# Keys stacked with their remainder, row statistics on ScalarE, and GpSimd's normalisation steps moved to the end of attention

## The reference

```python
x = x + tanh(g_xattn) * xattn(layernorm(x), ctx, Wq, Wk, Wv, Wout, bout)   # 32 x 256 tokens x 256, 8 heads of 64
x = x + tanh(g_ffn)   * ffn(layernorm(x), Wg, W1, W2, Ws1, Ws2)            # 16 experts, the best 2 of each token
# xattn, for each of the 32 batches and 8 heads; ctx is 77 x 192
sim  = (x @ Wq) @ (ctx @ Wk).T * 64 ** -0.5
out  = softmax(sim) @ (ctx @ Wv)                                            # then out @ Wout + bout
```

## Time and profile before

| | us |
|---|---|
| median of three runs | 1064.97 |
| the profiled execution's own time | 1065.26 |
| its span in the profile | 1063.4 |
| `prepare`, to the first score matmul | 34.5 |
| attention, to the first instruction of `mix` | 477 |
| `mix` and `passes` | 552 |

### The profile page before, as it was taken

The page is one execution under the profiler, slowest core; times in us unless marked ns, Lnnn a source line. Parts: engine busy times, 40 slices in busy tenths (PEclk is TensorE's granted clock), DMA queues, the critical chain, the costliest instruction groups (busy, mean ns, idle before and its releaser), DMA issues. The chain is left out here.

```text
span 1063.4 us, 21220 instructions
## 1 busy us (share of the span) xinstructions
PE 939.3 (88%) x6806; PEld 868.9 (82%) x6807; DVE 799.2 (75%) x1833; ACT 470.1 (44%) x965; POOL 518.6 (49%) x681
## 2 busy tenths in 40 slices
PE   4799999999999999899699999988887787887873
PEld 3699999999999999898588888876877775877873
DVE  5699999999999999867589898884565552665553
ACT  4456565556555555443454445531333231433331
POOL 7546454544536364634334555442455553355554
PEclk9799999999999999989899999999999999999997
DMA  8213232222323212211525444448899962766650
GB/s 222 69 44 98 86 98 83 66 79 86 98 86 98 69 53 65 66 54 51 169 74 180 161 170 160 159 164 275 295 310 309 314 213 99 250 202 217 207 169 13
DMA packets 108327, 150.95 MB, mean 142 GB/s; under 512 B 21830, under 2 KB 72394, under 8 KB 108240
## 3 DMA queue, kind: packets, MB, share of 16 engines
q1 hardware_dynamic: 92880, 107.60, 33.6%
q0 software_dynamic: 15360, 42.24, 10.5%
HBM read 90.19 MB, written 65.90 MB: 147 GB/s over the span
## 5 line engine op out<-in xcount | busy, mean ns | idle before, releaser
L639 POOL TENSOR_TENSOR prob<-prob,row_sum 128x616 f32<-128x616 f32 x64 | 78.0, 1219 | 127.4 <-DVE row_sum L846 127.0
L75 PE MATMUL ps_h<-w_flat,eyT_hi 128*128 x320 | 97.7, 305 | 34.2 <-DVE eyT_lo L1607 28.3
L1488 POOL DMA_INDIRECT rows_scratch<-prow x80 | 78.9, 986 | 86.1 <-DVE prow L1625 67.9
L1488 POOL DMA_INDIRECT out<-prow x80 | 78.9, 986 | 82.0 <-DVE prow L1625 62.6
L1582 ACT ACTIVATE eyT_hi<-ps_ey 128x512 fp32r<-128x512 f32 x80 | 48.2, 602 | 128.5 <-PE ps_ey L1510 102.0
L1075 POOL DMA_INDIRECT rows_scratch<-row,slot x64 | 67.7, 1058 | 76.0 <-DVE row L1326 61.3
L1625 DVE TENSOR_TENSOR prow<-ps_z,prow 128x512 f32<-128x512 f32 x80 | 54.9, 686 | 57.6 <-PE ps_z L77 39.8
L75 PEld LDWEIGHTS ps_h<-w_flat,eyT_hi 128*128 128x128 f32 x320 | 61.3, 192 | 40.9 <-issue 40.9
L76 PE MATMUL ps_h<-w_flat,eyT_hi 128*128 x320 | 90.3, 282 | 0.0
L77 PE MATMUL ps_h<-w_flat,eyT_lo 128*128 x320 | 90.1, 281 | 0.0
L249 POOL TENSOR_TENSOR xT_lo<-xT_raw,xT_hi 128x512 fp32r<-128x512 f32 x32 | 41.2, 1288 | 94.5 <-ACT ctxb_hi L215 93.4
(11 more groups left out here) (269 smaller groups left out, 3389.3 us busy)
## 6 DMA issues: line engine op xcount, KB each, us to landing
prow<-rows_scratch SPq DMA_DIRECT2D x160, 258.0 KB
rows_scratch<-blank SPq DMA_DIRECT2D x34, 258.0 KB, 2.8
xT_raw<-in_xT SPq DMA_DIRECT2D x32, 256.0 KB, 4.5
x_tok<-in_x SPq DMA_DIRECT2D x32, 256.0 KB, 2.9
x_scratch<-x_tok SPq DMA_DIRECT2D x32, 256.0 KB, 3.2
row<-x_scratch SPq DMA_DIRECT2D x16, 512.0 KB, 4.0
x_ahead<-in_x SPq DMA_DIRECT2D x26, 256.0 KB, 4.5
w_raw<-in_W SPq DMA_DIRECT2D x16, 256.0 KB, 3.4
```

What stands on the lines that cost most here:

```text
L75: nc.tensor.matmul(out, lh, rh, start=start and n == 0, stop=False)
L639: nc.gpsimd.tensor_tensor(pr, pr, row_sum[i][:, :].unsqueeze(2).broadcast_to((P, H, CK)), ALU.mult).then_inc(normed, 1)
L1488: pool.indirect_dma_start(dram, bass.IndirectOffsetOnAxis(target, 0), row[u][:, i, 0:columns], None, bounds_check=bound, oob_is_err=False) ...
```

## The change

1. **Stacked keys.** `kT[j]` holds, for head j of the pair, the high part in that head's 64 rows and the remainder in the other 64 rows. The high query weight is now present in both halves of the rows, so one matmul gives high by high plus high by low. The low query weight keeps its zeros and gives low by high. A unit is two matmuls instead of three.
2. **Keys split in halves.** `high_K` becomes two ScalarE copies of 64 x 308, and `low_K` two VectorE subtractions of 64 x 308.
3. **Weights in `prepare`.** ScalarE makes four 64 x 1024 copies into the high query weight where it made two; one of GpSimd's two zero fills goes.
4. **Row statistics on ScalarE.** The two `bn_stats` of a batch of x ahead go. ScalarE makes the negated mean with an accumulating Identity (after `high_OT`) and the sum of squares with an accumulating Square (after `high_PT(b,0)`), 2 of each in a batch. GpSimd's chain for these groups has 15 steps instead of 20.
5. **Second normalisation.** The 23 steps at the end of group 6 and the 23 at the end of group 7 become one run of 23 steps over 60 tiles, behind all of GpSimd's attention work.

```diff
@@ query_keys
-    products(nc, out, [
-        (c.wq_hi[:, h, cc * P:(cc + 1) * P], c.wq_lo[:, h, cc * P:(cc + 1) * P],
-         kT[0][:, :], kT[1][:, :])]).then_inc(a.M_done, 1)
+    h, cc, both = 2 * pair + k // 2, k % 2, kT[k // 2][:, :]
+    nc.tensor.matmul(out, c.wq_hi[:, h, cc * P:(cc + 1) * P], both, start=True, stop=False)
+    nc.tensor.matmul(out, c.wq_lo[:, h, cc * P:(cc + 1) * P], both, start=False, stop=True).then_inc(a.M_done, 1)
+def half(j):
+    return slice(j * DH, (j + 1) * DH)
+def high_keys(nc, a, kT, bank):
+    for j in range(2):
+        high(nc, kT[j][half(j), :], bank[half(j), :], a.K_hi)
+def low_keys(nc, v, a, n, kT, bank):
+    for j in range(2):
+        v.wait_ge(a.K_hi, 2 * n + j + 1)
+        low(nc, kT[j][half(1 - j), :], kT[j][half(j), :], bank[half(j), :], a.K_lo)
@@ make_M
-    pe.wait_ge(a.K_lo, n + 1)
+    pe.wait_ge(a.K_lo, 2 * n + 2)
@@ prepare, GpSimd
-                for w in (c.wq_hi, c.wq_lo):
-                    nc.gpsimd.memset(f32(w[:, :, :]), 0.0).then_inc(zeroed, 1)
+                nc.gpsimd.memset(f32(c.wq_lo[:, :, :]), 0.0).then_inc(zeroed, 1)
@@ prepare, TensorE
+                pe.wait_ge(wq_hi_done, 4)
                 pe.wait_ge(wq_lo_done, 2)
@@ prepare, ScalarE
-                act.wait_ge(zeroed, 2)
                 act.wait_ge(centred, 4)
-                for j in range(2):
-                    high(nc, head_rows(c.wq_hi, j), wq_raw[j * DH:(j + 1) * DH, :, :], wq_hi_done)
+                for at in (0, 1):
+                    for j in range(2):
+                        high(nc, head_rows(c.wq_hi, j, j ^ at), wq_raw[half(j), :, :], wq_hi_done)
@@ attend, GpSimd, body
                     if exists(g + 2):
                         pool.wait_ge(ahead_stats, 2 * GB * (g + 1))
-                        rstd_of(2 * GB * (g + 2), 2 * GB, LN_STEPS * (g + 1))
-                    else:
-                        part = g - (GROUPS - 2)
-                        begin, end = 0 if part == 0 else known2, known2 if part == 0 else TILES - LATE_TILES
-                        pool.wait_ge(x1_stats, end)
-                        norm_of_stats(nc.gpsimd, linked(pool, rstd_chain, LN_STEPS * (GROUPS - 1) + NORM_STEPS * part),
-                                      c, begin, end - begin, var2[:, 0:end - begin], work2[:, 0:end - begin])
+                        tiles = slice(2 * GB * (g + 2), 2 * GB * (g + 3))
+                        rstd_of_squares(nc.gpsimd, linked(pool, rstd_chain, LN_STEPS + LN_AHEAD_STEPS * g),
+                                        squares[:, tiles], c.rstd1[:, tiles], var1[:, 0:2 * GB], work1[:, 0:2 * GB])
+                        pool.sem_inc(rstd_ready, 1)
@@ attend, GpSimd, behind the groups
+                pool.wait_ge(x1_stats, known2)
+                norm_of_stats(nc.gpsimd, linked(pool, rstd_chain, LN_STEPS + LN_AHEAD_STEPS * (GROUPS - 2)), c, 0, known2, var2[:, :], work2[:, :])
@@ attend, ScalarE
+                def mean_ahead(b, b_half, par):
+                    act.wait_ge(a.ahead_in[par], 16 * (b_half + 1))
+                    for i in range(2):
+                        t = 2 * (b + 2 * GB) + i
+                        nc.scalar.activation(unused[i][:, :], a.x_ahead[par][:, i, :], ACT.Identity, scale=-1.0 / D,
+                                             accum_out=less_mean[:, t:t + 1]).then_inc(ahead_mean, 1)
+                def squares_ahead(b, par):
+                    wait(act, ahead_stats, 2 * b)
+                    for i in range(2):
+                        t = 2 * (b + 2 * GB) + i
+                        act.wait_ge(ahead_mean, 2 * b + i + 1)
+                        nc.scalar.activation(unused[2 + i][:, :], a.x_ahead[par][:, i, :], ACT.Square,
+                                             bias=less_mean[:, t:t + 1],
+                                             accum_out=squares[:, t:t + 1]).then_inc(ahead_stats, 1)
...
                         if not (first and q == 0):
                             high_OT(b - 1)
+                        if exists(g + 2):
+                            mean_ahead(b, 2 * g + q // 2, q % 2)
                         if not last:
                             high_M_units(b, g, q, 1)
                         exponentials(b, 1)
                         high_PT(b, 0)
+                        if exists(g + 2):
+                            squares_ahead(b, q % 2)
@@ attend, VectorE: stats_ahead and its two calls in a batch
-                    nc.vector.bn_stats(a.stats1[:, bass.ds((2 * (b + 2 * GB) + i) * 6, 6)],
-                                       a.x_ahead[par][:, i, :]).then_inc(ahead_stats, 1)
```

More of the change, by code:

```diff
@@ L106 @@
 LN_STEPS = 6 + 2 + 3 * 4
+LN_AHEAD_STEPS = 1 + 2 + 3 * 4
 NORM_STEPS = LN_STEPS + 3
@@ L120, in linked, with newton @@
     return link
+def newton(g, link, rstd, var, work):
+    link(g.tensor_scalar(rstd.bitcast(I32), var.bitcast(I32), -0.5, float(SEED), ALU.mult, ALU.add))
+    link(g.tensor_scalar(var, var, -0.5, None, ALU.mult))
+    for _ in range(3):
+        link(g.tensor_tensor(work, rstd, rstd, ALU.mult))
+        link(g.tensor_tensor(work, work, var, ALU.mult))
+        link(g.tensor_scalar(work, work, 1.5, None, ALU.add))
+        link(g.tensor_tensor(rstd, rstd, work, ALU.mult))
 def rstd_by_newton(g, link, stats, rstd, var, work):
@@ L130, in rstd_by_newton, with rstd_of_squares @@
     link(g.tensor_tensor(var, var, work, ALU.add))
[L131 to L137, removed]
+    newton(g, link, rstd, var, work)
+def rstd_of_squares(g, link, squares, rstd, var, work):
+    link(g.tensor_scalar(var, squares, 1.0 / D, LN_EPS, ALU.mult, ALU.add))
+    newton(g, link, rstd, var, work)
 def norm_of_stats(g, link, c, first, tiles, var, work):
@@ L155, in attention_tensors @@
     a.ctxM = [sb("ctxM_hi", [P, 2, GK], F32R), sb("ctxM_lo", [P, GK], F32R)]
-    a.kT = [sb(f"kT_{s}", [P, GK], F32R) for s in ("hi", "lo")]
+    a.kT = [sb(f"kT_{j}", [P, GK], F32R) for j in range(2)]
     a.ctxb_raw = [sb(f"ctxb_raw{i}", [P, 2, CK]) for i in range(2)]
@@ L289, in high_K @@
     wait(act, a.M_done, 4 * n)
-    high(nc, a.kT[0][:, :], a.ps_proj[1][:, 0:GK], a.K_hi)
+    high_keys(nc, a, a.kT, a.ps_proj[1][:, 0:GK])
 def low_K(nc, v, a, n):
-    v.wait_ge(a.K_hi, n + 1)
-    low(nc, a.kT[1][:, :], a.kT[0][:, :], a.ps_proj[1][:, 0:GK], a.K_lo)
+    low_keys(nc, v, a, n, a.kT, a.ps_proj[1][:, 0:GK])
 def M_out(a, s, parity, cc, h):
@@ L334, in prepare @@
         bank_M = [ps(f"ps_m{i}", [P, 512])[:, 0:GK] for i in range(4)]
-        kT = [a.kT, [sb(f"kT2_{s}", [P, GK], F32R) for s in ("hi", "lo")]]
+        kT = [a.kT, [sb(f"kT2_{j}", [P, GK], F32R) for j in range(2)]]
         wq_raw = sb("wq_raw", [P, 4, D])
@@ L354, in by_batch, with head_rows @@
             return bank.rearrange("p (b k) -> p b k", b=GB)
-        def head_rows(w, j):
-            return w[j * DH:(j + 1) * DH, :].rearrange("p (q j) d -> p q j d", j=2)[:, :, j, :]
+        def head_rows(w, j, at=None):
+            return w[half(j if at is None else at), :].rearrange("p (q j) d -> p q j d", j=2)[:, :, j, :]
         with nc.Block(no_gpsimd_drain=True) as block:
@@ L430, in key_unit @@
                 def key_unit(n):
-                    wait(pe, a.K_lo, n - 1)
+                    wait(pe, a.K_lo, 2 * (n - 1))
                     keys(nc, c, a, bank_K[n % 2], n)
                 def query_key_units(n):
-                    pe.wait_ge(a.K_lo, n + 1)
+                    pe.wait_ge(a.K_lo, 2 * n + 2)
                     for k in range(4):
@@ L466, in high_key @@
                     wait(act, a.M_done, 4 * (n - 1))
-                    high(nc, kT[n % 2][0][:, :], bank_K[n % 2] if n < 4 else a.ps_proj[1][:, 0:GK], a.K_hi)
+                    high_keys(nc, a, kT[n % 2], bank_K[n % 2] if n < 4 else a.ps_proj[1][:, 0:GK])
                 def high_query_keys(n):
@@ L499, in _ @@
                                             ALU.subtract, ALU.mult).then_inc(centred, 1)
+                v.wait_ge(zeroed, 1)
                 for j in range(2):
@@ L512, in low_key @@
                 def low_key(n):
-                    v.wait_ge(a.K_hi, n + 1)
-                    low(nc, kT[n % 2][1][:, :], kT[n % 2][0][:, :], bank_K[n % 2] if n < 4 else a.ps_proj[1][:, 0:GK],
-                        a.K_lo)
+                    low_keys(nc, v, a, n, kT[n % 2], bank_K[n % 2] if n < 4 else a.ps_proj[1][:, 0:GK])
                 def low_query_keys(n):
@@ L554, in attend @@
         var1, work1 = sb("var1", [P, 4 * GB]), sb("work1", [P, 4 * GB])
+        less_mean, squares = sb("less_mean", [P, TILES]), sb("squares", [P, TILES])
+        unused = [sb(f"unused{i}", [P, D], BF16) for i in range(4)]
         ps_proj = a.ps_proj
@@ L572, in attend @@
         x1_done, x1_stats = sem("x1_done"), sem("x1_stats")
-        ahead_stats, rstd_chain, rstd_ready = sem("ahead_stats"), sem("rstd_chain"), sem("rstd_ready")
-        known2 = 2 * GB * (GROUPS - 2)
+        ahead_mean, ahead_stats, rstd_chain, rstd_ready = (
```

(2 more changed lines are left out.)

14 lines of the change are left out of this document (5 added, 9 removed).

## The result

| | before | changed |
|---|---|---|
| median | 1063.33 us (1060.57 to 1066.9, 4 runs) | 1052.16 us (1051.0 to 1053.72, 4 runs) |
| ratio, 95% interval | | 0.9897 [0.9864, 0.993] |
| the profiled execution, its span | 1065.26, 1063.4 | 1053.72, 1051.7 |

The change gains 11.2 us. The forecast was 20.6, and 1052.16 lies just past the range's high end of 1052.

What follows compares the result with a forecast made beforehand. TensorE's sum of starts was taken to bound attention, VectorE close behind. Units -15.4, batch 28 -6.0 and start +0.8 gave -20.6 us from 1065.26: 1044.7, stated as 1044.5 for the median; range 1040 to 1052.

Steps and rivals of the forecast that it cites:

- the second adds 0.39: VectorE's key split in attention: the second subtraction costs 0.39 us a batch, lower bound half of that.
- without them it is 4.78 us: VectorE between a batch's two `row_max`: 5.40 us less TensorE-caused waits is 4.78; 0.28 late, with 0.33 in hand.
- Rival (a): Attention loop: VectorE becomes the bound, loop 14.0 to 14.2 us, 4 to 10 us of gain lost, 1049 to 1054; chance 0.12.
- TensorE shows idle time before `attend_values`: Sign in the attention loop's profile that the forecast is wrong and VectorE has become the bound; no size given.
- Part 1: Attention units on TensorE: two matmuls instead of three save 0.573 us a batch, giving TensorE alone a 13.84 us period.
- Part 4: Row statistics on ScalarE in attention: both pairs, 1.1 us each, fit holes of 1.90 and 2.29 us; cost 0.
- rival (b): ScalarE's accumulating activations cost double: loop 14.4 us in 24 batches, 12 us lost, 1057 us; chance 0.04.
- Rival (d): ScalarE in attention: a table load at each turn between Exp and Square, 1075 us or some 1106; chance 0.04.
- The removal is worth nothing now: VectorE in attention: dropping the two `bn_stats` a batch gains nothing, as their cost lay in idle time.
- Part 5: Batch 28: with the normalisation chain gone it falls from 18.92 to 12.90 us, 6.0 us saved.
- rival (c): Batch 28's boundary wait stays, because `norm(28,0)` is late for another reason: 1050.7 us; chance 0.04.
- +0.8: Start, in `prepare`: five second key subtractions on VectorE cost between 0 and 1.9 us, taken as 0.8.

Runs made afterwards that it cites:

- halves in place: Changed kernel with both half-height key subtractions writing a spare tile in the rows they read, so remainders miss the products: 991.69 us, batch 13.99.
- same-rows version: Changed kernel with both key subtractions on rows 0 to 63 into two spare tiles, so no key remainder reaches the products: 981.93 us, batch 13.85.
- GpSimd moving the halves: Changed kernel with one full-height VectorE key subtraction, four half copies on GpSimd, statistics steps spread over three batches: 1038.91 us, batch 13.84.
- first group: Four runs of the change in parts, three rounds, sharing one chip with runs of the kernel before, which took 1007.73 us there.
- part 5 alone: Kernel before with only the single 60-tile normalisation chain behind GpSimd's attention work: 1001.15 us, ratio 0.9957, batch 28 at 12.83 us.

## Why the prediction was wrong

**Failed: part 2, "the second adds 0.39".** The term was mis-sized; it had a bound below (half of it) and none above, and the truth lay above. I argued from durations by columns, which are right (0.47 for 64 x 308), but the price of an instruction is the distance of starts, and that rests on the overlap with its neighbours. The pair and its neighbours take 0.75 more than the one subtraction did, not 0.39: worked out from the table, 0.39 for the second instruction and 0.36 for three lost overlaps. In `prepare` it can be read directly, between the same neighbours, first in the kernel before and then in the changed one:

```profile
25.74 0.41 DVE L509 BATCH_NORM_STATS2 stats<-xs 128x6 f32<-128x256 f32 x1
26.07 0.46 DVE L220 TENSOR_TENSOR kT_lo<-ps_k,kT_hi 128x308 fp32r<-128x308 f32 x1
26.45 0.74 DVE L534 TENSOR_SCALAR wo_raw<-wo_raw,tanh_g 128x1024 f32<-128x1024 f32 x1
```

```profile
27.69 0.42 DVE L537 BATCH_NORM_STATS2 stats<-xs 128x6 f32<-128x256 f32 x1
28.14 0.98 DVE L232 TENSOR_TENSOR kT<-ps_k,kT 64x308 fp32r<-64x308 f32 x2
29.15 0.75 DVE L560 TENSOR_SCALAR wo_raw<-wo_raw,tanh_g 128x1024 f32<-128x1024 f32 x1
```

From `bn_stats` to what follows the keys it is 0.71 us with one subtraction and 1.46 with two. In the loop, the own time of the second half is 9.12 us measured, 8.99 forecast; the rest of that half was 0.23 less than I had (8.99 + 0.36 - 9.12), so the two errors partly cancel.

**Failed: part 2, "without them it is 4.78 us".** I took the first half of the batch as VectorE's own work and let it end 0.28 late at the batch's start and catch up. It can't catch up: the scores of the second rows stand in TensorE's queue behind `attend_values`, which waits for VectorE's `PT_lo`. So when VectorE is late, the scores are late too. The distance stays at 5.02 with 0.34 of waiting in it (279.91 + 0.68 = 280.59, `attend_values` at 280.64, `row_max` at 285.53). My "0.33 in hand" were not to be had. The loop that sets the period now is `PT_lo`, `attend_values`, the second scores, VectorE's second half, `PT_lo`: 5.02 + 9.12 = 14.14, against TensorE's 13.84. With 5.0 for the first half, 13.84 leaves VectorE's second half 8.84, and the forecast's own 8.99 was already over that. The run with halves in place shows it: its second half takes just 8.99 us, and yet a batch takes 13.99 and not 13.84. So this step alone would have spoiled the forecast by 0.15 a batch, and the mis-sized pair adds the last 0.13. The shown price of the base rows fits: where only they change, from the same-rows version to the in-place one, the batch goes from 13.85 to 13.99.

**Rival (a) was right and had 0.12.** Its reason, "the spare of 0.07 is less than the uncertainty", was sound, and weighed too little. Its range of 14.0 to 14.2 us held the 14.12 of a batch. Batches 1 to 27 gained 9.2 us where the forecast had 27 x 0.55 = 14.9.

**The sign was not to be read as I wrote.** "TensorE shows idle time before `attend_values`" was to prove rival (a); none is shown, and TensorE is busy for 14.14 of 14.14. The distance of 0.27 between two starts is the sign.

**Part 1 was right.** Units of two matmuls, 0.57 us less for TensorE; with GpSimd moving the halves the whole of it comes through, at 13.84.

**Part 4 was right in its cost, 0** (14.44 with and without it, three matmuls a unit), with one more instruction than expected. ScalarE's groups in the changed kernel:

```profile
L828 ACT ACTIVATE unused<-x_ahead,less_mean 128x256 bf16<-128x256 f32 x48 | 23.8, 500 | 0.0
L819 ACT ACTIVATE unused<-x_ahead 128x256 bf16<-128x256 f32 x48 | 19.4, 408 | 0.0
L828 ACT ACTIVATION_READ_ACCUMULATOR unused<-x_ahead,less_mean 128x1 f32 x48 | 9.3, 193 | 0.0
L819 ACT ACTIVATION_READ_ACCUMULATOR unused<-x_ahead 128x1 f32 x48 | 9.2, 192 | 0.0
...
L227 ACT ACT_TABLE_LOAD x1 | 1.3, 1283 | 0.8 <-PEq L1741 0.8
L1250 ACT ACT_TABLE_LOAD x1 | 1.3, 1283 | 5.4 <-PEq L623 5.4
```

The pair of means takes 0.9 us and that of squares 1.08, for the 1.1 forecast. The read of the accumulator is an instruction of its own, as rival (b) feared, but of 0.19 us, not 0.6. Rival (d) falls: two table loads in all, as before, so Square runs under the table that is loaded for Exp. What I missed is part 4's worth. "The removal is worth nothing now" holds for the kernel before; with parts 1 to 3 it is worth 0.14 us a batch (14.26 to 14.12), 3.2 in batches 1 to 23 by the traces.

**Part 5 was right**, to 0.02 us: 6.02 for 6.0, and rival (c) falls. GpSimd's chain over 60 tiles and VectorE's last `bn_stats`:

```profile
483.32 0.37 POOL L137 TENSOR_TENSOR work<-stats 128x60 f32<-128x60 f32 x1
...
492.25 0.31 POOL L159 TENSOR_TENSOR shift<-shift,rstd 128x60 f32<-128x60 f32 x1
```

```profile
496.30 0.43 DVE L907 BATCH_NORM_STATS2 stats<-x_tok 128x6 f32<-128x256 f32 x1
```

The chain takes 9.2 us (I allowed 10.9) and ends 4.2 before attention does. In the first group part 5 alone gained 6.6 us in all.

**Failed in size: the start, "+0.8".** The first `row_max` came 3.28 later. Part of that is when the first loads land: the first key subtraction started between 14.8 and 16.7 us over the runs. From VectorE's first key subtraction to the first linked step of GpSimd it was 18.60 us before, 18.42 and 17.37 in the two runs with whole keys, and 20.1 to 21.2 in the nine with stacked ones: about 2.5 more. VectorE's own stretch, from its first key subtraction to the last `bn_stats` of `prepare`, grew from 17.15 to 20.25, by 3.1 us, where the forecast had 1.9 at most. It is the same mis-sized term, five times.

**Not foreseen: batch 0**, -2.35. In both kernels TensorE was granted 1.2 GHz, the lower level, for a part of this batch, and the batch's mean is the same. What differs is where that part lies. The batch's stretch and its first transposes, before and changed:

```profile
37.80:53.59 15.79, 12.12 (x64) 10.50 (x63) 10.84 (x21) 7.86 (x16) 7.88 (x16) 0.78 0.29 81
45.32 1.99 PE L722 MATMUL ps_pt<-ident,prob 128*77 128x128 f32 x8 [1.84 <-POOL prob L639]
```

```profile
41.08:54.51 13.43, 11.33 (x60) 9.79 (x60) 10.68 (x19) 9.61 (x25) 7.62 (x16) 0.77 0.32 92
48.35 1.10 PE L747 MATMUL ps_pt<-ident,prob 128*77 128x128 f32 x8 [1.11 <-POOL prob L668]
```

Before, TensorE had waited 1.84 us for the probabilities, the clock was low from 44.3 to 51.1, and from these transposes to the scores of batch 1 it took 6.29 us (45.32 to 51.61). In the changed kernel the low part came down from `prepare` and ended at 47.2, before the transposes, and the same work took 4.19 (48.35 to 52.54). These 2.1 us are most of the 2.35. What decides where the low part falls was not tried. So this gain was luck: no term of the forecast holds it, and it hides most of the miss at the start.

**By the terms:** -9.2 for the loop (forecast -14.9), -6.0, +3.3 - 2.35 at the start (forecast +0.8 - 0.5), +0.2 in the tail of attention, +2.5 scatter behind it: -11.6, for the span's -11.7.

## What to carry to other kernels

When an edit brings a second engine to within 1% of the bound, the forecast hangs on that engine's spacing of starts, so price each added instruction with what it does to the overlap of its neighbours, and ask whether it changes the base row. Draw the loop that runs through both queues before you grant one engine slack: lateness that comes back through the other can't be made up. And give moved work to an engine whose queue has room at that very point; its busy share does not tell.

## What the runs showed of the hardware

- On VectorE two 64 x 308 subtractions from the same base row start 0.38 us apart; when the base row changes between 0 and 64, 0.48 to 0.51. The durations shown hardly differ, 0.45 to 0.48.
- ScalarE looks alike, though no run varied it: two 64 x 308 copies of 0.42 us, of rows 0 to 63 and then 64 to 127, start 0.45 apart in the changed kernel, the second 25 ns after the end of the first. Its 77 x 512 copies, of 0.57 to 0.59 us and from the same base row, start 0.47 apart.
- An accumulating activation over 128 x 256 is 0.41 (Identity) or 0.50 us (Square), and a read of 0.19 behind it, of which about half overlaps with the next.
- GpSimd copies 64 x 308 to other rows in 0.44 us; ScalarE takes 0.46 for that copy, and VectorE's subtraction of the same shape 0.47.
- A wait of TensorE of up to about 0.16 us is not shown as idle (an estimate: a 308-column matmul is given 0.30 us and takes 0.14). Distances of starts show it.
